# Evictions, exponentials and the last batch's filter put in another order in an attention and expert layer

## The reference, cut to what matters

```python
xn = layernorm(x)                              # x: 16 batches x 256 tokens x 128
# attention, 16 heads of 8
q = xn @ Wq + bq; lat = xn @ Wl + bl; k = lat @ Wk + bk; v = lat @ Wv + bv
attn = softmax(q k^T / sqrt(8)) @ v
a = attn @ Wo + bo
# expert layer, 8 heads with a query of 2 x 16
f = batchnorm(xn @ fWq + fbq)
s0, s1 = l2norm(f halves) . l2norm(key0), l2norm(key1)      # 32 scores each
top 4 of s0 x top 4 of s1 -> 16 pairs, softmax over them -> w, idx
eh = gelu(expert_down[idx] . xn);  m = sum(expert_up[idx] * (eh * w))
out = x + a + m
```

## Time and profile before

| engine | busy us | share of span | instructions |
|---|---|---|---|
| PE (matmul) | 301.2 | 89% | 3189 |
| DVE | 310.5 | 92% | 1381 |
| ACT | 277.2 | 82% | 509 |
| POOL | 265.6 | 79% | 542 |

### The profile page before, as it was taken

How to read it: one execution, slowest core, us unless ns; L and a number is a source line. 1 busy time by engine, 2 the same in 40 slices (tenths; PEclk the granted TensorE clock), 3 DMA queues, 4 the chain that set the end, 5 groups by cost and what they waited for, 6 DMA issues and landing times.

```text
span 337.4 us, 9964 instructions
## 1 busy us (share of the span) xinstructions
PE 301.2 (89%) x3189; PEld 168.2 (50%) x3189; DVE 310.5 (92%) x1381; ACT 277.2 (82%) x509; POOL 265.6 (79%) x542
## 2 busy tenths in 40 slices
PE   7999999977898989898988988988989898988786
PEld 3555554353455555545454545554545555455445
DVE  6599999899899999999999999999999999999781
ACT  3699986988687978888888888888888797888881
POOL 7289886825958898989898989898888889898930
PEclk9899999999799999999999999999999999999999
DMA  4765665417021212212140404030403030000001
GB/s 124 215 166 160 173 183 164 109 56 129 27 77 27 71 58 59 73 41 85 31 108 7 111 5 111 3 114 4 111 21 93 22 94 18 4 19 2 19 17 31
DMA packets 45888, 24.83 MB, mean 74 GB/s; under 512 B 5452, under 2 KB 45708, under 8 KB 45836
## 3 DMA queue, kind: packets, MB, share of 16 engines
q1 hardware_dynamic: 45836, 24.20, 26.5%
HBM read 15.54 MB, written 8.39 MB: 71 GB/s over the span
## 4 chain that ended last, share of the span: by engine, by line
PE 50%; ACT 19%; DVE 15%; issue 11%; POOL 3%; ACTq 0%; POOLq 0%; DVEq 0%
PE bank L734 12%; PE bank L763 8%; PE SJ L714 5%; PE bank L756 5%; ACT Eb L473 4%; PE SI L673 4%; ACT s_sb L393 3%; DVE top L1098 3%; PE bank L791 3%; DVE negm L1072 2%; ACT order L485 2%; PE bank L792 2%; ACT onT L456 2%; PE SI L587 2%; ACT Osb L440 1%
## 5 line engine op out<-in xcount | busy, mean ns | idle before, releaser
L1072 DVE TENSOR_REDUCE negm<-SI 128x4 f32<-128x1024 f32 x128 | 152.2, 1201 | 1.2 <-PE SI L673 1.2
L473 ACT ACTIVATE Eb<-SJ 128x1024 f32<-128x1024 f32 x117 | 119.2, 1019 | 9.4 <-PE SJ L714 9.3
L734 PE MATMUL bank<-Eb,vhat 128*18 128x256 f32 x1024 | 68.1, 383 | 11.2 <-ACT s_sb L393 10.3
L1377 POOL TENSOR_TENSOR prod<-r_sb,a 128x1024 f32<-128x1024 f32 x28 | 53.5, 1912 | 0.0
L1098 DVE MAX8 top<-s_sb 128x8 f32<-128x32 f32 x480 | 47.5, 177 | 6.0 <-ACT s_sb L393 6.0
L714 PE MATMUL SJ<-QS,KS 50*128 50x256 bf16 x484 | 48.0, 274 | 4.7 <-ACT Eb L473 4.7
L673 PE MATMUL SI<-KS,QS 48*128 48x256 bf16 x512 | 50.9, 273 | 0.3 <-DVE negm L1072 0.3
L734 PEld LDWEIGHTS bank<-Eb,vhat 128*18 128x18 f32 x1024 | 24.0, 97 | 37.7 <-ACT s_sb L393 14.2
L1111 DVE MATCH_REPLACE8 r_sb<-top,s_sb 128x36 f32<-128x36 f32 x240 | 40.5, 181 | 0.0
L673 PEld LDWEIGHTS SI<-KS,QS 48*128 48x128 bf16 x512 | 21.2, 94 | 27.9 <-issue 22.2
L763 PE MATMUL bank<-cst,prod 128*128 128x128 f32 x240 | 32.8, 280 | 0.0
(11 more groups left out here) (227 smaller groups left out, 632.5 us busy)
## 6 DMA issues: line engine op xcount, KB each, us to landing
qk_parts<-parts SPq DMA_DIRECT2D x48, 128.0 KB, 2.4
QS<-qk_parts SPq DMA_DIRECT2D x32, 96.0 KB
KS<-qk_parts SPq DMA_DIRECT2D x32, 96.0 KB
x_sb<-L_attn_x SPq DMA_DIRECT2D x8, 256.0 KB, 4.1
QS<-qk_parts SPq DMA_DIRECT2D x32, 64.0 KB
KS<-qk_parts SPq DMA_DIRECT2D x32, 64.0 KB
out<-ysb SPq DMA_DIRECT2D x16, 128.0 KB, 2.0
QS<-qk_parts SPq DMA_DIRECT2D x32, 32.0 KB
```

The costliest lines, as they stand in the source:

```text
L473: A(Eb[:, n % 4, :], SJ[:, :], ACT.Exp).then_inc(s["ex"], 1)
L734: last = mm(psO[32 * c:32 * c + 2 * VC, (q % 2) * S:(q % 2 + 1) * S], vhat[:, v0:v0 + 2 * VC], Eb[:, (2 * g + c // 2) % 4, e0:e0 + S], sta ...
L1072: V.tensor_reduce(negm[:, bb % 2, :, :, pr].rearrange("p t e -> p e t"), SI[slot % 2][:, :].rearrange("p (e t j) -> p e t j", e=2, j=S), a ...
L1377: TT(prod[:, t, :, :, :], r_sb[:, hs, 0:NK].unsqueeze(2).to_broadcast([P, FH, TOP, NK]), a0[:, hs, :].unsqueeze(3).to_broadcast([P, FH, TO ...
```

## The change

It edits four engines' lists, in the loop and in the tail.

- **Loop, ACT.** The eviction of outputs that stood at `k` = 1 is now at `k` = 0, after that slot's exponential and in front of `mT`; the one at `k` = 5 stays. The exponential of 512 columns of `z_sb` moves from `k` = 6 to the end of `k` = 7.
- **Loop, POOL.** `split_maxima` of the last batch is moved from `k` = 7 to the middle of the ranks of batch 14.
- **Tail, DVE and ACT.** Batch 15's marked scores get their own place `r_last`; `match_replace` no longer waits for POOL's products. The best-four copies go from POOL to ACT, the scaling of `z_sb` from POOL to DVE, the two exponentials of `z_sb` become one of 704 columns, the masking is split in two halves and stands after `normalised(LB - 1)`, the input is added on DVE instead of by four identity matmuls and two ACT evictions.
- **Tail, PE and ACT order.** `sj`, `values`, `turn_products`, `turn_outputs`, `turn_heads` and the evictions are interleaved otherwise; `finish` of batch 14 comes behind the turned heads of batch 15.

```diff
@@ ScalarE, loop
-                if m >= 0 and m % 4 == 0 and m // 4 < 2 * B:
-                    ... the eviction of Osb
+                if m >= 0 and k == 5:
+                    heads_out(m // 4)
...
+                if k == 0 and m >= -1:
+                    heads_out((m + 1) // 4)
                 if k == 0 and 0 <= b < B:
                     act.wait_ge(s["mt"], b + 1)
...
                     A(ties, ties, ACT.Identity, bias=one, scale=-1.0).then_inc(s["eq"], 1)
+                if k == 7 and 0 <= b < B:
                     act.wait_ge(s["z"], b + 1)
                     A(z_sb[:, :, 0:NK], z_sb[:, :, 0:NK], ACT.Exp).then_inc(s["z1e"], 1)
@@ ScalarE, tail
             finished(LB - 2, in_bank)
+            weights(N0)
             last_scores(0)
             A(mT[:, :], psM[0:2 * H, 0:S], ACT.Copy).then_inc(s["mt_ev"], 1)
-            weights(N0)
             last_scores(1)
+            outputs(2 * LB - 2)
             weights(N0 + 1)
-            outputs(2 * LB - 2)
-            for n in range(N0 + 2, N0 + 5):
+            weights(N0 + 2)
+            best_four(LB, 0)
+            best_four(LB, 1)
+            for n in range(N0 + 3, N0 + 6):
                 weights(n)
             outputs(2 * LB - 1)
-            weights(N0 + 5)
-            act.wait_ge(s["zs"], B)
-            A(z_sb[:, :, NK:ZW], z_sb[:, :, NK:ZW], ACT.Exp).then_inc(s["ze"], 1)
             act.wait_ge(s["z"], B)
-            A(z_sb[:, :, 0:NK], z_sb[:, :, 0:NK], ACT.Exp).then_inc(s["z1e"], 1)
+            A(z_sb[:, :, :], z_sb[:, :, :], ACT.Exp).then_inc(s["ze"], 1)
...
             weights(N0 + 9)
+            weights(N0 + 10)
             heads_turned(LB - 1, psM[:, 0:S], onT)
-            weights(N0 + 10)
             outputs(2 * LB + 1)
             heads_turned(LB, psP, onT_last)
-            finished(LB - 1, in_bank)
-            finished(LB, psY)
@@ TensorE, tail
+            sj(N0)
             scores(LB, (0, 1), psS)
-            sj(N0)
             turn_maxima(LB)
...
             turn_products(0, psM)
             sj(N0 + 4)
+            values(4 * LB - 1)
             sj(N0 + 5)
-            values(4 * LB - 1)
+            sj(N0 + 6)
             turn_products(1, psM)
-            sj(N0 + 6)
-            turn_outputs(LB - 1, psM)
+            sj(N0 + 7)
             values(4 * LB)
-            sj(N0 + 7)
             sj(N0 + 8)
             values(4 * LB + 1)
+            turn_outputs(LB - 1, psM)
             sj(N0 + 9)
-            turn_heads(LB - 1, psM)
             sj(N0 + 10)
             values(4 * LB + 2)
+            turn_heads(LB - 1, psM)
+            values(4 * LB + 3)
             pe.wait_ge(s["last_pr"], 2)
             turn_products(0, psT)
-            values(4 * LB + 3)
+            turn_outputs(LB, psC)
             turn_products(1, psT)
-            turn_outputs(LB, psC)
+            turn_heads(LB, psP)
+            finish(LB - 1)
             for t in range(BT):
                 mm(psY[:, t, :], wgT_last[:, t * P:(t + 1) * P], up_sb[:, :], start=True, stop=False)
-                mm(psY[:, t, :], ident, x_sb[:, BT * LB + t, :], start=False, stop=False)
-            turn_heads(LB, psP)
-            finish(LB - 1)
@@ VectorE, tail
+            def with_input(b, src):
+                V.tensor_tensor(ysb[:, b % 2, :, :], src, x_sb[:, BT * b:BT * (b + 1), :], ALU.add)
-                dve.wait_ge(s["pr"], 4 * LB - 2 * (1 - t))
-                    last = V.match_replace(r_sb[:, h, :], top4[:, h, :], s_last[:, h, 1, :], NEG)
+                    last = V.match_replace(r_last[:, h, :], top4[:, h, :], s_last[:, h, 1, :], NEG)
+            V.tensor_tensor(z_sb[:, :, NK:NK + TOP], first, each(0, TOP), ALU.mult)
+            V.tensor_tensor(z_sb[:, :, NK + TOP:ZW] ..., top8[:, :, :, 0:TOP], rb ..., ALU.mult)
+            V.tensor_tensor(z_sb[:, :, 0:NK], s_last[:, :, 1, 0:NK], each(1, NK), ALU.mult).then_inc(s["z"], 1)
...
             normalised(LB - 1, psM)
+            masked(0)
+            masked(1)
@@ GpSimd
                     TT(rank[:, 0, :, :], cm2[:, :, :, 0], cm2[:, :, :, 1], ALU.add).then_inc(s["rk"], 1)
+                    if b == LB - 1:
+                        split_maxima(LB)
```

More of the change, by code:

```diff
@@ L400, in best_four, with heads_out @@
                 A(half(top4[:, :, 0:TOP], e), half(top8[:, :, 1, 0:TOP], e), ACT.Copy).then_inc(s["t4"], 1)
+            def heads_out(q):
+                act.wait_ge(s["pv"], 2 * q + 2)
+                if q >= 2:
+                    act.wait_ge(s["ct"], q // 2)
+                A(Osb[:, q % 2, :], psO[:, (q % 2) * S:(q % 2 + 1) * S], ACT.Copy).then_inc(s["o_ev"], 1)
             for slot in range(NSLOT):
@@ L531, in finished @@
                 act.wait_ge(s[f"st{b % 2}"], 16 * (b // 2))
-                A(ysb[:, b % 2, :, :], src, ACT.Copy).then_inc(s["y_ev" if b < LB - 1 else "last_fin"], 1)
+                A(ysb[:, b % 2, :, :], src, ACT.Copy).then_inc(s["y_ev"], 1)
             in_bank = psM[:, 0:S].rearrange("p (t d) -> p t d", d=D)
             finished(LB - 2, in_bank)
+            weights(N0)
             act.wait_ge(s["pad2"], 1)
@@ L791, in finish @@
                     mm(psM[:, t * D:(t + 1) * D], onT[:, t * P:(t + 1) * P], wo_sb[:, :], start=True, stop=False)
-                    last = mm(psM[:, t * D:(t + 1) * D], wgT[:, t * P:(t + 1) * P], up_sb[:, :], start=False, stop=(b < LB - 1))
-                    if b == LB - 1:
-                        last = mm(psM[:, t * D:(t + 1) * D], ident, x_sb[:, BT * b + t, :], start=False, stop=True)
+                    last = mm(psM[:, t * D:(t + 1) * D], wgT[:, t * P:(t + 1) * P], up_sb[:, :], start=False, stop=True)
                 last.then_inc(s["y"], 1)
@@ L1147, in normalised @@
                                 ALU.mult).then_inc(s["on"], 1)
[L1149 to L1155, removed]
+            def with_input(b, src):
+                dve.wait_ge(s["y"], b + 1)
+                dve.wait_ge(s[f"st{b % 2}"], 16 * (b // 2))
+                dve.wait_ge(s["xb"], 4)
+                V.tensor_tensor(ysb[:, b % 2, :, :], src, x_sb[:, BT * b:BT * (b + 1), :], ALU.add).then_inc(s["last_fin"], 1)
+            dve.wait_ge(s["z1e"], LB)
+            dve.wait_ge(s["mr"], 4 * LB)
+            V.scalar_tensor_tensor(r_sb[:, :, 0:NK], r_sb[:, :, 0:NK], NEG, z_sb[:, :, 0:NK],
+                                   ALU.is_equal, ALU.mult).then_inc(s["es"], 1)
             dve.wait_ge(s["sel"], LB)
@@ L1204, in _, with masked @@
             V.reciprocal(dd[:, :], both).then_inc(s["fe"], 1)
+            dve.wait_ge(s["tie"], LB + 2)
+            for i, (lo, n, at) in enumerate(((1, 3, 0), (2, 2, 3), (3, 1, 5))):
+                dve.wait_ge(s["rk"], 4 * LB + i + 1)
+                V.tensor_tensor(rank[:, 0, :, lo:TOP], rank[:, 0, :, lo:TOP], ties[:, :, at:at + n], ALU.add).then_inc(s["rk"], 1)
+            dve.wait_ge(s["rk"], 4 * LB + 4)
+            V.tensor_scalar(rank[:, 1, :, :], rank[:, 0, :, :], float(TOP), None, ALU.is_lt).then_inc(s["sel"], 1)
+            def masked(t):
+                hs = slice(FH * t, FH * (t + 1))
+                dve.wait_ge(s["mr"], 4 * LB + 2 * (t + 1))
+                V.scalar_tensor_tensor(r_last[:, hs, 0:NK], r_last[:, hs, 0:NK], NEG, z_sb[:, hs, 0:NK],
+                                       ALU.is_equal, ALU.mult).then_inc(s["es"], 1)
             normalised(LB - 1, psM)
+            masked(0)
+            masked(1)
             dve.wait_ge(s["fa"], B)
-            dve.wait_ge(s["es"], B)
+            dve.wait_ge(s["es"], B + 1)
             dve.wait_ge(s["wt"], 2 * LB)
@@ L1289, in normalised, with split_maxima @@
                    ALU.mult).then_inc(s["on"], 1)
+            def split_maxima(b):
+                pool.wait_ge(s["mx"], NPAIR * (b + 1))
+                if b >= 1:
+                    pool.wait_ge(s["mt"], b)
+                most = negm[:, b % 2, :, :, :]
+                V.tensor_copy(mpart[:, :, :, 0, :], most).then_inc(s["mh"], 1)
+                pool.wait_ge(s["mh"], b + 1)
+                TT(mpart[:, :, :, 1, :], most, mpart[:, :, :, 0, :], ALU.subtract).then_inc(s["ms"], 1)
             for slot in range(NSLOT):
@@ L1341, in _ @@
                     V.tensor_scalar(rank[:, 1, :, :], rank[:, 0, :, :], float(TOP), None, ALU.is_lt).then_inc(s["sel"], 1)
-                bm = slot // 8
-                if k == 7 and bm < B:
-                    pool.wait_ge(s["mx"], NPAIR * (bm + 1))
-                    if bm >= 1:
-                        pool.wait_ge(s["mt"], bm)
-                    most = negm[:, bm % 2, :, :, :]
-                    V.tensor_copy(mpart[:, :, :, 0, :], most).then_inc(s["mh"], 1)
-                    pool.wait_ge(s["mh"], bm + 1)
-                    TT(mpart[:, :, :, 1, :], most, mpart[:, :, :, 0, :], ALU.subtract).then_inc(s["ms"], 1)
+                if k == 7 and slot // 8 < LB:
+                    split_maxima(slot // 8)
                 if k == 7 and 0 <= b < B:
@@ L1403, in _ @@
```

(15 more changed lines are left out.)

48 lines of the change are left out of this document (23 added, 25 removed).

## The result

The changed kernel takes 330.69 us (median of four runs, 330.68 to 330.77), the kernel before 339.32 us beside it (four runs, 337.73 to 340.84): a ratio of 0.9747, 95% interval 0.9701 to 0.9792. I had predicted 332.3 with a range of 330.0 to 335.8. The profiled execution took 330.68 us with a span of 328.9; before it was 339.15 and 337.4, so the two traces differ by 8.5 us.

The account below looks back on a forecast made before the run. DVE was taken to bound the kernel, with a hand-over costing a third of a microsecond per batch. Loop 3.8 + 1.0 = 4.8 us plus tail 2.0 gave 6.8 off 339.15: 332.3 us, range 330.0 to 335.8.

Parts of the forecast that it names:

- DVE becomes the only limit: Rival, loop: DVE alone sets the period; 14 x 0.4 = 5.6 us plus a tail of 2.4, time 331.1; chance 0.10.
- `Osb` ahead of `mT`: Loop, ACT: earlier eviction removes PE's 0.27 us wait before the filter scores; 14 x 0.27 = 3.8 us, bounds 0 and 6.2.
- Large exponential in slot 7: Loop, ACT: `onT` and `finish` come 0.15 us earlier; 0.08 us in 13 periods, 1.0 us, bounds 0 and 2.0.
- the slower rival: Loop, ACT: the moved exponential delays the filter scores, up to 0.52 us in 14 batches, 7.3 us; 339.7; chance 0.05.
- DVE as next limit: Loop: the period was to fall from 15.99 to 15.6 to 15.7 us, with DVE alone allowing 15.55.
- POOL as third limit: Loop: POOL's 0.29 us wait ahead of `z_sb` shrinks to almost nothing; POOL is late next, not yet the limit.
- The tail: After the loop: reordered work and batch 15's earlier maxima gain 2.1 us, taken as 2.0.
- the start of the last exponential: Tail, ACT: the last exponential starts at 325.33 us, 1.8 us earlier.
- from there to the last add: Tail end: 7.13 us instead of 7.51, the final add on DVE taking about 0.04 more than the eviction.
- The stretch of ACT: Tail, exponentials `weights(N0 + 4)` to `weights(N0 + 10)`: 7.14 us instead of 8.19, starting at 318.19, 0.74 earlier.
- the first product turned on PE: Tail, PE: no longer behind one more `values` and `sj`, this step comes at 316.8 instead of 317.47, gain 0.67.
- The port: Tail: DVE's two-operand instructions may stop POOL at a shared SBUF port; gain then 1.8 us instead of 2.1.

Follow-up runs that it names:

- the padded kernels: Three unused MAX8 per batch added on DVE: to the kernel before, 341.54 us, period 16.14; to the kernel after, 336.77 us, period 15.85.
- e1_loop: Kernel before with only the loop part (`Osb` evicted ahead of `mT`, large exponential at the end of slot 7), old tail; 333.05 us, period 15.57.
- e4_tail: Kernel after with ACT's loop order put back to that of before, new tail and batch 15 maxima kept; 336.57 us, period 15.98.
- e11: Kernel after with `sj(N0 + 4)`, `values(4 LB - 1)`, `sj(N0 + 5)` before batch 14's first turned product, and DVE's MAX8 wait set on `s_tie`; 330.32 us.
- e9_add_last: Kernel after with POOL's addition of the input for batch 13 moved behind batch 15's probabilities; 330.52 us.
- e2_outputs_first: Kernel before with only the eviction of `Osb` moved ahead of `mT`; 333.89 us, period 15.64.
- e6_after_pad: Kernel after with three more unused MAX8 per batch on DVE; 336.77 us in one run, period 15.85.
- e12_maxima_back: Kernel after with batch 15's maxima split where the kernel before does it, behind batch 14's ranks on POOL; 330.69 us in one run.
- e7_warm: Kernel after with five unused bf16 matmuls of 512 columns on PE in the tail's two waits; 331.42 us.

## Why the prediction was right, step by step

The course that I held likeliest happened in its mechanism, but its main term came out larger: the loop went all the way to the rival "DVE becomes the only limit", whose 331.1 us lie closer to the measured 330.69 than my 332.3. The rest of the agreement is partly luck, as the last paragraph of this section shows.

- *`Osb` ahead of `mT`*: 0.27 us per batch predicted, 0.35 measured alone. The mechanism holds: PE's wait is gone in every batch. The bound of 0.44 from DVE's reduce was the better guide to what could be won than the wait that PE showed. Why 0.08 more than that wait came is not traced.
- *Large exponential in slot 7*: 0.08 predicted on top, 0.14 measured alone and 0.07 on top. It covers ACT's 0.34 us wait; the slower rival, 0.52 us a batch on the way to the filter scores, did not occur in any trace.
- *DVE as next limit*: I had 15.6 to 15.7 for the period and named 15.55 for DVE alone. It came to 15.57, and the padded kernels show DVE as the limit. The rival "DVE becomes the only limit" is thus what the loop did: 13 periods at 0.42 are 5.5 us, and with the last stretch (0.26 by e1_loop) 5.7, where the sum had 4.8 and the rival 5.6.
- *POOL as third limit*: its 0.29 us wait ahead of `z_sb` was to shrink to almost nothing, and did. No trace shows another engine waiting for it there.
- *The tail*: 2.0 us predicted. With the clock steady, e4_tail has 2.3 us from the loop's last `mT` on, 2.1 of them behind the tail's own. Two of its terms were off in opposite directions: up to the start of the last exponential 1.5 us were won, not 1.8, and from there to the last add 0.7, not 0.34. The stretch of ACT that I had added up to 7.14 us took 7.19; what was late was its start, because the first product turned on PE came 0.5 us earlier and not 0.67. Where I wrote that start as 318.19, my terms add up to 318.15. The profiled kernel after shows only 0.34 us behind the tail's `mT`, and 0.45 in front of it from the maxima, since the clock fell at 309 us. The prediction had left that fall out, and it had not counted the copy of the last maxima by DMA (PE waits 0.72 us for it).
- *The port*: I priced it at 0.3 us in the tail. It is there (POOL's last sum 1.18 us), and DVE waits 0.18 us for it; in e11 0.73.

The sum against the two traces: the loop won 5.7 us, a steady clock at 86 to 90 us about 0.6 (by difference), the clock at 8 to 12 us 1.4, and the tail (0.3 + 0.45) what the fall of its clock left. Some 2 us of the 8.5 are thus clock that the change did not touch, and 1.6 it did not get. That these two nearly cancel is luck. Without either the stretches make it about 8 us. Whole executions at full clock make it less: 336.96 against 329.72 and 330.20 us (e9_add_last, about 0.3 us slower in its tail than the kernel after would be), so 6.8 to 7.2 us, or some 7.5 at most with that 0.3 added; and the two parts alone, e1_loop and e4_tail, 5.5 + 1.5 = 7.0. The forecast was 6.8. No execution of the kernel after itself had its clock at full throughout, so between 7 and 8 us the value stays open.

## What to carry to other kernels

Find in the period the shortest wait of the busiest engine (here DVE's 0.33 us) and follow it back over each in-order hand-over: an eviction that can run earlier in a wait of its own engine is free, and what it frees is at most the busiest engine's idle time, counted to where the instruction before would have let the next one start (0.44 us here, of which 0.42 were won). Once nothing is left of it, only work taken off that engine shortens the loop. To see whether an engine is the limit, give it a little more work: all of it shows in the period only if it is (0.28 of 0.28 us after, 0.15 of 0.28 before). When a few microseconds count, compare periods and stretches of the trace at the same clock, not medians alone.

## What the hardware did unexpectedly

TensorE's granted clock fell in some executions and not in others at a few places of the same code (8 to 12, 74 to 80 and 86 to 90 us, and in the tail: 309 to 313 us in the kernel after, 314 to 317 in e2_outputs_first with the old tail). After nearly the same two waits, of 0.7 and 0.9 us, it fell once (after) and twice not (e6_after_pad, e9_add_last). A fall costs 1.4 us in the prologue, 1.5 to 1.6 us in the tail, and at 74 to 80 us 0.9 (the first two periods of `mT` together take 34.26 us in e12_maxima_back and 33.40 in the kernel after). Runs of the kernel before spread over 336.96 to 341.01 us, and the one at 336.96 has its clock at full.

Not every slow stretch shows in the granted clock. In e2_outputs_first, e6_after_pad and e7_warm the first `mT` starts at 71.8 us, where the kernel after has 68.65, though the granted clock reads 1.00 up to 72 us. Their matmuls before 14 us take up to nearly twice as long, here the same group in the kernel after and in e7_warm:

```profile
7.58 1.25 PE L616 MATMUL SI<-onT 128*128 128x512 bf16 x5
```
```profile
8.41 2.31 PE L616 MATMUL SI<-onT 128*128 128x512 bf16 x5
```

Why is not shown. It is worth 3.1 us, more than any single fall, and none of these prologues was edited.

Two VectorE and GpSimd instructions that both read two SBUF operands hold each other up: 2.07 us for 0.73, 0.77 for 0.20 and 0.62 for 0.17.
